# A gather-scatter GNN kernel: the message stream in five parts instead of seven

## The reference

```python
edge_index = jnp.stack([src, dst])
h = jnp.maximum(_layernorm(x, axis=-1), 0.0)
x = x + _L0_gnn_ref(h, edge_index, ...)    # mean of h[src] per dst, two products, log_softmax
h = jnp.maximum(_layernorm(x, axis=-1), 0.0)
x = x + _L1_gnn_ref(h, edge_index, edge_attr_64, ...)

# _L1_gnn_ref
weight = jnp.maximum(edge_rbf @ W1 + b1, 0.0) @ W2 + b2
h = x @ Wl + bl
msg = h[col] * weight                      # row = src, col = dst
out = jax.ops.segment_sum(msg, row, num_segments=x.shape[0])
```

## Time and profile before

| | us |
|---|---|
| times of three runs | 3461.6, 3456.3, 3461.3 |
| median | 3461.3 |
| span of the profiled execution (all that is recorded of its time) | 3469.3 |
| PE busy in it | 2987.6 |
| DVE busy | 2757.6 |
| ACT busy | 2085.3 |
| POOL busy | 1808.5 |

### The profile page before, as it was taken

The page is one execution under the profiler, slowest core; times in us unless marked ns, Lnnn a source line. Parts: engine busy times, 40 slices in busy tenths (PEclk is TensorE's granted clock), DMA queues, the critical chain, the costliest instruction groups (busy, mean ns, idle before and its releaser), DMA issues.

```text
span 3469.3 us, 97235 instructions
## 1 busy us (share of the span) xinstructions
PE 2987.6 (86%) x26330; PEld 2437.6 (70%) x26331; DVE 2757.6 (79%) x7718; ACT 2085.3 (60%) x4907; POOL 1808.5 (52%) x1790
## 2 busy tenths in 40 slices
PE   0799999999668878899999989988889898998977
PEld 0699999999655556776766666766667666766766
DVE  8899999999786657777777777777777777777866
ACT  2599999998353335555555545555455555555656
POOL 3400010000127777667766676666766677677750
PEclk9999999999868889999999999999999999999999
DMA  3198888960103336666666656655666666666657
GB/s 117 37 326 313 311 309 310 311 213 3 38 19 107 103 103 172 179 175 160 178 164 161 160 150 172 166 162 147 166 168 180 165 158 184 173 158 175 181 154 207
DMA packets 506188, 593.04 MB, mean 171 GB/s; under 512 B 71050, under 2 KB 477058, under 8 KB 505905
## 3 DMA queue, kind: packets, MB, share of 16 engines
q1 hardware_dynamic: 449506, 470.49, 49.4%
q0 software_dynamic: 56400, 119.07, 9.9%
HBM read 293.94 MB, written 295.35 MB: 170 GB/s over the span
## 4 chain that ended last, share of the span: by engine, by line
DVE 36%; PE 32%; issue 17%; DVEq 7%; DMA 4%; POOL 2%; ACT 1%; SPq 0%; POOLq 0%; ACTq 0%
PE PS L1119 11%; DVE X L1017 8%; PE PS L1110 5%; DVE big L990 4%; PE PS L1282 4%; PE PS L1249 4%; DMA messages<-big,idxr 4%; DVE big L978 3%; DVE aux L768 3%; DVEq L1012 3%; DVE big L964 2%; DVE big L975 2%; DVE big L967 2%; DVE hpar L1006 2%; PE PS L1261 2%
## 5 line engine op out<-in xcount | busy, mean ns | idle before, releaser
L605 POOL DMA_INDIRECT messages<-big,idxr x1664 | 1637.0, 984 | 720.8 <-issue 466.5
L1282 PE MATMUL PS<-big,hpar 128*128 128x128 f32 x5120 | 663.8, 283 | 163.7 <-DVE hpar L1006 128.7
L1282 PEld LDWEIGHTS PS<-big,hpar 128*128 128x128 f32 x5120 | 610.5, 195 | 223.1 <-DVE hpar L1006 181.2
L1432 ACT ACTIVATE big<-PS,b1c 128x512 f32<-128x512 f32 x416 | 286.0, 688 | 708.3 <-PE PS L1238 708.3
L1017 DVE TENSOR_TENSOR X<-X,PS 128x128 f32 x1280 | 368.7, 288 | 325.3 <-PE PS L1282 131.9
L1119 PE MATMUL PS<-h_parts,counts 128*128 128x258 f32 x3626 | 565.3, 296 | 0.0
L1359 ACT ACTIVATE counts<-PS 128x784 fp32r<-128x784 f32 x592 | 481.7, 825 | 93.9 <-PE PS L1110 85.6
L1249 PE MATMUL PS<-W2s,big 128*128 128x128 f32 x3328 | 500.8, 295 | 0.0
L1249 PEld LDWEIGHTS PS<-W2s,big 128*128 128x128 f32 x3328 | 419.0, 197 | 98.3 <-issue 98.3
L1119 PEld LDWEIGHTS PS<-h_parts,counts 128*128 128x128 f32 x3626 | 470.2, 191 | 0.2 <-ACT counts L1359 0.2
L1443 ACT ACTIVATE big<-PS 128x512 f32<-128x512 f32 x416 | 247.6, 595 | 347.2 <-PE PS L1261 339.4
(11 more groups left out here) (222 smaller groups left out, 3639.1 us busy)
## 6 DMA issues: line engine op xcount, KB each, us to landing
messages<-zeros SPq DMA_DIRECT2D x896, 193.5 KB
big<-messages SPq DMA_DIRECT2D x320, 516.0 KB
aux<-slot_rows SPq DMA_DIRECT2D x416, 128.0 KB
big<-in_edge_attr_dram SPq DMA_DIRECT2D x402, 128.0 KB
messages<-big,idxr POOLq DMA_INDIRECT x1664
X<-in_x_dram SPq DMA_DIRECT2D x12, 448.0 KB, 6.9
out_dram<-X SPq DMA_DIRECT2D x6, 448.0 KB
edge_places<-big SPq DMA_DIRECT2D x1, 2496.0 KB, 13.2
```

The lines of the kernel that those rows point to most:

```text
L605: pool.indirect_dma_start(strm_d, bass.IndirectOffsetOnAxis(ap=idxr[:, n % U, j:j + 1], axis=0), outr[:, n % U, j, :], None).then_inc(S_sc ...
L1282: last = nc.tensor.matmul(to[:, r * C:(r + 1) * C], finhot[:, n % 2, r * 2 + q, :], fin[:, k, r, q * ROW:q * ROW + C], start=(q == 0), sto ...
```

## The change

Two tables of numbers, nothing else:

```diff
-    LOOPS = ((3, 4), (5, 2), (4, 4), (4, 4), (3, 4), (5, 2), (2, 2))
-    EVERY = (1, 4, 5, 6)
+    LOOPS = ((7, 4), (6, 4), (4, 4), (3, 4), (3, 2))
+    EVERY = (2, 3, 4)
```

## The result

The changed kernel takes 3484.0 us in the median of four runs (3481.7 to 3497.3), the kernel before 3461.5 beside it: a ratio of 1.0071, 95% interval 1.005 to 1.0092. A second measurement, with another set of runs, gave 3485.0 against 3466.9, ratio 1.0047 (1.0034 to 1.006). The forecast was 3465, range 3452 to 3482.

What follows compares the result with a forecast made beforehand. Part 0 was taken to go at POOL's pace, later loops at PE's, with stops at edges of large loops. Stream -1.4, tail +9.4 and chain -4 made +4 us on 3461.3: 3465, range 3452 to 3482.

Steps and rivals of the forecast that it cites:

- Term 1: Part 0's loop: 64 groups more at POOL's pace of 5.07 us a group, 324.7 us, together 568.2.
- Term 5: Part 3's loop of 48 full groups: same as today's, 297.9 us.
- Term 3: Part 1's loop: 96 groups in six rounds, three sum steps in four groups, inner rounds 91.4 us each, 542.5 us.
- Term 2: Switches between parts: four in place of six, 61.8 us for the first and 58.4 for each other, 237.1 us.
- Terms 4 and 6: Full loops: part 2's 64 groups in four rounds, 399.4 us; part 4's 24 groups in three 8-group rounds, 143.2 us.
- Term 7: Tail after the stream: 40 sum steps in place of 36, hidden by nothing, +9.4 us.
- Term 8: DVE's chain between count stage and layer 0: two of six split rounds fall away, -4 us (gain 1.5 to 7).
- The slower one: Edges of the 8-group loop, perhaps part 0's, begin to stall: 3477 us, up to 3488; chance 0.14.
- as the count of work says: Part 0 is not held by POOL and its 64 added groups run at 3.94 us: 3393 us; chance 0.04.
- The faster one by edges: Some five of ten stalling loop edges stop no more, 25 us less: 3440 us (3420 to 3455); chance 0.12.
- loops stop at the edge by the size of their body: Message-stage loops: rounds of 16 groups with sum steps stall at each edge, 6.0 us if full, 4.0 otherwise; 8-group loops don't.
- The prediction's own sign of being wrong: Wrong if part 0 falls below 4.8 us a group, 16-group rounds leave 91 and 101 by over 2, or count stage moves.

Runs made afterwards that it cites:

- e3: The changed kernel with two of the four scatters of each group left out, so half of the messages are missing from the sums; 3329.6 us.
- e4: The kernel before with the same two of four scatters of each group left out; 3377.3 us.
- e9: The changed kernel with four one-column matmuls (8 instructions) on PE ahead of the message stage, moving PE's later code; 3478.4 us, against 3485.0 unmoved beside it.
- e6: The changed kernel with part 0's loop in 28 rounds of 4 groups instead of 7 of 16, later loops only moved; 3474.2 us.
- e8: The kernel before with its four loops of full groups in rounds of 4 groups; 3473.5 us, ratio 1.0033.
- e1: The changed kernel with the full loops of parts 2 and 3 in rounds of 8 groups instead of 16; 3462.5 us, ratio to the kernel before 0.9998.
- b1: New plan of five parts, three loops with sum steps in two of four groups, rounds of 8 groups; 3443.8 us, ratio to the kernel before 0.9943.
- e10: b1 with 64 one-element memsets on DVE ahead of the message stage, moving DVE's later code by 64 places; 3400.4 us, ratio to the kernel before 0.9802.
- e5: The changed kernel with all three loops of full groups in rounds of 4 groups; 3460.0 us, ratio to the kernel before 0.999.

## Why the prediction was wrong

**Term 1, part 0 at POOL's pace: right.** 568.3 against 568.2, the waits for landed scatters 83.7 against 85, and e3 and e4 show the mechanism and its worth.

**Term 5, part 3's loop "as today's": the largest miss.** 305.9 against 297.9. The body is the same as that of part 4 before, but lies elsewhere. PE stops twice at its edges, and the half clock behind the stop lasts 13.6 us in place of 6.7. e9 and e6 show that it is a matter of place.

**Term 3, part 1's loop: 7.3 too low.** I took inner rounds at the mean of two of today's, 91.4; they took 92 to 93.8. In e8 the same loops range from 359.7 to 368.0 for four rounds by place alone. But the excess here was not moved by either move of the code: the loop takes 549.4 us in e6 and 549.3 in e9. The traces show one thing more. The queue q8, which went with PE's code in e9, loads next to nothing in this loop, 6 transfers in six rounds, against 33 and 16 in the four rounds of each of the two loops before. PE's longest wait in it:

```profile
PE PS L1282 <- DVE hpar L1006: 47.8, 34, 5.3
```

PE's body is still held here and PE has no stop of its own; at each edge it waits for DVE's one-hots, behind DVE's stop of 3.0 to 3.9 us. The rounds are no shorter for it. Why they are 1.3 us longer than before stays open.

**Term 2, switches: 3.8 too low,** most of it in the first (65.0 and in five other runs of this plan 63.5 to 66.3, against 61.8). No run was made for it, but with half of the scatters the first switch takes 55.2 us in the change and 54.6 before (e3, e4), so its excess goes with the scatters. Terms 4 and 6 were right within 3 us (4 was 2.9 too high).

**Term 7, the tail: right,** 9.4 for four steps; from the last message to the end it is 8.4.

**Term 8, the chain: right in itself,** -3.3 against -4. The Trainium skill's rule that the prediction named ("SBUF — State Buffer", section "SBUF: two separate sides") agrees with the trace: the add behind the split, with one input in PSUM, takes 0.42 us at 902.38, inside POOL's stretch. The upper end of the gain was not reached even so, since three instructions were still held and L778 came into POOL's stretch and lost 1.0. In the total the gain is hard to see: the first message comes between 1031.9 and 1042.1 in seven profiles of the new plan, between 1036.7 and 1039.8 in three of the old.

**The rivals.** The slower one had the right mechanism and side, at 0.14, and its span (3477 up to 3488) holds the measured time; that is luck, for it named the wrong edges. The 8-group loop did not begin to stop in the change. The edges that stopped already came to stop for longer. The 8-group stops that it named appeared in e1 and b1. The faster rival "as the count of work says" is refuted by part 0 at 5.07 a group and by e3 and e4. The faster one by edges came about in half, on PE in part 1, and saved nothing, since DVE stopped at the same edges. No run has a 16-group loop with sum steps in which both engines go on; e10 shows such a gain for a body of 8 groups alone.

**The step that failed** is "loops stop at the edge by the size of their body", priced as a constant of 4 and 6 us an edge. It made the stream -1.4 us; measured are +15.3, of which part 3's loop is 8.0 over its term (shown to be of place), part 1's loop 7.3 (open) and the switches 3.8 (open), with part 2's 2.9 the other way. The prediction's own sign of being wrong came true: rounds of 16 groups differ from 91 and 101 by more than 2 (93.8 and 105.7 at most). I had the rule for the place in hand and gave it a rival's chance instead of a width on ten edges. Against rounds without a stop (95.4 us for 16 full groups, 87.4 with three sum steps in four) an edge costs 4.3 to 10.3 us in the full loops and 2.3 to 6.7 in the others, its slow start included. By my estimate that is some 20 us of uncertainty for ten edges, and the range should have gone to 3490 at least.

The Trainium skill ("Runtime: NRT & Kernel Launch", "Instruction fetch mechanics") speaks of blocks of 256 instructions, of which most engines hold two, and of a fetch when a taken branch leaves them. The runs agree in what they can show. By the traces' records, DVE's body of 8 full groups has 304 instructions, and stopped in e1 and b1 but not in the change and in e10. With 4 groups (154) no stop is seen, as in e5, and those of 16 groups with sum steps (604, or 535 with three in four) stopped in each kernel that had one. Part 0's body of 16 groups (328) stopped in none.

So the change is slower for this reason: the sum steps it saves are worth nothing where they were saved, because POOL holds part 0; the tail takes 8 to 9 us more; and the stops at edges cost more, by more edges in rounds of 16 and, in part 3, by longer stops.

## What to carry to other kernels

Work taken from an engine counts only in stages where the others wait for it: price a change by each stage's floor, and then put work where an engine has room under that floor. Here half-rate loops, at 5.2 us a group close to POOL's 5.07, brought 3400 to 3404 us, 1.7 to 2.0% below the kernel before. A loop whose body doesn't fit where it lies stops at each edge; before comparing two plans, bring bodies to a size that never stops (here rounds of 4 groups), or the comparison is of code placement. The transfers of kind "instruction" in the DMA table tell whether a loop loads its code again in each round.

## What the runs showed of the hardware that was not expected

64 memsets ahead of the loops, 1.2 us of DVE's time in all, made a kernel 43 us faster (3443.8 to 3400.4), and eight instructions on PE took one of two stops (3.1 and 4.5 us) from each edge of a loop. After a stop of 4.3 us PE's clock is granted at half (1.2 of 2.4 GHz) for 6.7 us, after one of 8.5 us for 13.6: the eight passes of L1249 take 2.08 instead of 1.16 us, and this is part of an edge's price. Idle time costs clock in a whole stage too: part 0's mean granted clock was 0.82 with all the scatters, where PE waited for POOL, and 1.00 with half of them.
